# Message passes of a graph network: a subtraction split over two engines, gathers spaced by arithmetic, one root for two norms

## The reference, cut to what matters

```
for l in range(3):
    m = concat([x[dst], x[src], edge_features])
    m = relu(layernorm(m @ msg_w1[l] + msg_b1[l]))
    m = relu(layernorm(m @ msg_w2[l] + msg_b2[l]))
    agg = segment_sum(m, dst)
    x = x + relu(layernorm(concat([x, agg]) @ upd_w[l] + upd_b[l]))
```

## Time and profile before

| | |
|---|---|
| Device time, median of 3 runs | 12204.72 us (12200.19 to 12210.75) |
| Span of the profiled execution | 10931.0 us |
| Busy: TensorE, VectorE, ScalarE, GpSimd | 68%, 58%, 57%, 68% of the span |
| The three message passes, from the span's start | about 3215 to 4375, 4735 to 5830, 6200 to 7275 us |

### The profile page before, as it was taken

One profiled execution on the slowest core, in us unless ns is written; L12 is line 12 of the kernel. 1 busy time (PEld: TensorE's weight loads), 2 busy tenths in 40 slices (PEclk: granted clock), 3 DMA queues, 4 the chain that ended last, 5 costly groups with the idle time before them and its releaser, 6 DMA issues. The chain is left out here.

```text
span 10931.0 us, 359225 instructions
## 1 busy us (share of the span) xinstructions
PE 7478.6 (68%) x118837; PEld 6235.2 (57%) x118838; DVE 6352.6 (58%) x16271; ACT 6235.4 (57%) x16925; POOL 7430.6 (68%) x9327
## 2 busy tenths in 40 slices
PE   6666666555687777777777877767777756445666
PEld 5444444344576666766666766656666643443465
DVE  7444444455438888357774477763488887116543
ACT  2555555555449999368884488862499966003200
POOL 2777777777558887468885588860288854773576
PEclk8555555555699999899998999989999989668877
DMA  6222222189996666675555855559966649887998
GB/s 239 69 65 70 69 66 69 60 291 320 270 330 204 202 203 182 251 248 170 170 168 176 306 170 170 170 86 373 345 201 201 201 146 394 259 259 271 358 331 251
DMA packets 1258845, 2290.57 MB, mean 210 GB/s; under 512 B 293739, under 2 KB 691324, under 8 KB 1231742
## 3 DMA queue, kind: packets, MB, share of 16 engines
q1 hardware_dynamic: 913886, 1129.25, 32.5%
q0 software_dynamic: 232416, 575.55, 17.9%
q10 hardware_dynamic: 112320, 582.80, 13.1%
HBM read 1381.15 MB, written 905.59 MB: 209 GB/s over the span
## 5 line engine op out<-in xcount | busy, mean ns | idle before, releaser
L639 POOL DMA_INDIRECT by_src<-sort_rec,slots x1560 | 1540.9, 988 | 651.2 <-issue 650.9
L1312 POOL DMA_INDIRECT NEAR<-spread_f,gather_ids_l x1368 | 1322.5, 967 | 336.9 <-issue 252.8
L1387 ACT ACTIVATE z_l<-z_l,stat_l 128x64 f32<-128x64 f32 x5472 | 1438.0, 336 | 0.0
L773 PE MATMUL bank<-hots_t 104*128 104x512 bf16 (+3 forms) x1568 | 612.6, 466 | 722.0 <-ACT junk L598 721.7
L1475 PE MATMUL bank<-m_l,NEAR 128*128 128x64 bf16 x5472 | 559.0, 193 | 517.7 <-issue 391.4
L1475 PEld LDWEIGHTS bank<-m_l,NEAR 128*128 128x128 bf16 x5472 | 492.8, 97 | 561.8 <-issue 552.5
L1321 POOL TENSOR_TENSOR rest_l<-m_l 128x512 f32<-128x512 f32 x684 | 716.0, 1047 | 140.5 <-DVE m_l L1375 130.7
L1487 PE MATMUL bank<-wm_diag,zr_t_l 128*128 128x128 f32 x5472 | 807.3, 291 | 0.0
L773 PEld LDWEIGHTS bank<-hots_t 104*128 104x128 bf16 x1568 | 217.3, 139 | 1021.0 <-ACT junk L598 833.8
L1487 PEld LDWEIGHTS bank<-wm_diag,zr_t_l 128*128 128x128 f32 x5472 | 674.9, 194 | 156.8 <-issue 156.8
L1301 POOL TENSOR_TENSOR piece_l<-rest_l 128x512 bf16<-128x512 f32 x684 | 710.9, 1039 | 59.9 <-POOL rest_l L1321 12.2
(11 more groups left out here) (379 smaller groups left out, 25591.5 us busy)
## 6 DMA issues: line engine op xcount, KB each, us to landing
spread_f<-unit_rows_a ACTq DMA_DIRECT2D x342, 512.0 KB, 5.8
hot_t_l<-dst_hots_t SPq DMA_DIRECT2D x456, 256.0 KB
NEAR<-dst_hots SPq DMA_DIRECT2D x456, 256.0 KB, 3.2
unit_hot_a<-src_hots_t SPq DMA_DIRECT2D x342, 256.0 KB, 4.1
spread<-sum_unit_rows ACTq DMA_DIRECT2D x114, 768.0 KB
spread<-last_unit_rows ACTq DMA_DIRECT2D x114, 768.0 KB
dst_hots<-NEAR SPq DMA_DIRECT2D x228, 256.0 KB, 2.5
dst_hots_t<-hot_t_l SPq DMA_DIRECT2D x228, 256.0 KB, 2.1
```

Of the source, the lines that this page charges most:

```text
L639: pool.indirect_dma_start(out=by_src, out_offset=bass.IndirectOffsetOnAxis(ap=slots[h][:, j:j + 1], axis=0), in_=rec[h][:, j, :], in_offse ...
L773: pe.matmul(to, lhsT=cols[:, t * P:width], rhs=cols[:, 0:width], start=True, stop=False, skip_group_check=True)
L1312: pool.indirect_dma_start(out=far_in[h % WA][:, g * GT:(g + 1) * GT, :].rearrange("p j f -> p (j f)"), out_offset=None, in_=spread_f, in_o ...
L1387: last = act.activation(z[h % WA][:, t, :], z[h % WA][:, t, :], ACT.Relu, scale=stat[h % WA][:, 2, t:t + 1])
```

## The change

In `mpnn_pass` alone:

- `piece2` is split by columns: VectorE does the first 256 (4 tiles), between the second norm's sum and the keys, GpSimd the other 256. TensorE waits for both.
- GpSimd's order becomes gather, half of `piece2`, ids, gather, `rest`.
- The sums of both norms go to one array `sizes`; one root and one reciprocal a tick serve the first norm of lag 4 and the second norm of lag 8. VectorE's reciprocal at the head of the tick goes. The array's second column is set to 1.0 ahead of the pass.

```diff
 GpSimd
+                        if p := part(0):
+                            h, st, n, nth = p
+                            if h % WA == 0:
+                                pool.wait_ge(s["ids"], 2 * nth - (h < WA))
+                            at_least(pool, s["z"], n - WA)
+                            pool.sem_inc(turn, 1)
+                            gather(h, 0)
                         if p := part(9):
                             h, st, n, nth = p
                             pool.wait_ge(s["rest"], n)
                             at_least(pool, s["acc_ps"], n - 2)
-                            pool.tensor_tensor(piece2[h % 2][:], rest[h % 2][:], top(rest[h % 2]),
+                            pool.tensor_tensor(piece2[h % 2][:, LOW:, :], rest[h % 2][:, LOW:, :], top(rest[h % 2])[:, LOW:, :],
                                                ALU.subtract).then_inc(s["piece2"], 1)
                         if p := part(0):
                             h, st, n, nth = p
-                            if h % WA == 0:
-                                pool.wait_ge(s["ids"], 2 * nth - (h < WA))
-                            at_least(pool, s["z"], n - WA)
                             if h % WA == WA - 1 and not (isinstance(st, int) and st + 1 >= steps):
                                 take_ids(1 - h // WA, st + 1)
                             pool.sem_inc(turn, 1)
-                            for g in range(2):
-                                pool.indirect_dma_start(
...
+                            gather(h, 1)
 VectorE
+                    for k in range(WA):
+                        dve.memset(sizes[k][:, 0, 1, :], 1.0).then_inc(s["sized"], 1)
+                    dve.wait_ge(s["sized"], WA)
...
-                        if p := part(5):
-                            h, st, n, nth = p
-                            dve.wait_ge(s["root1"], n)
-                            dve.reciprocal(stat[h % WA][:, 2, :], stat[h % WA][:, 1, :]).then_inc(s["rec1"], 1)
...
                         if p := part(8):
                             h, st, n, nth = p
                             dve.wait_ge(s["square2"], n)
-                            dve.tensor_reduce(stat[h % WA][:, 3, :], vv[:], AX, ALU.add).then_inc(s["sum2"], 1)
+                            dve.tensor_reduce(sizes[h % WA][:, 0, 1, :], vv[:], AX, ALU.add).then_inc(s["sum2"], 1)
+                        if p := part(9):
+                            h, st, n, nth = p
+                            dve.wait_ge(s["rest"], n)
+                            at_least(dve, s["acc_ps"], n - 2)
+                            dve.tensor_tensor(piece2[h % 2][:, 0:LOW, :], rest[h % 2][:, 0:LOW, :], top(rest[h % 2])[:, 0:LOW, :],
+                                              ALU.subtract).then_inc(s["piece2_v"], 1)
...
+                        if p := norms(part):
+                            h, k, n = p
+                            dve.wait_ge(s["root"], k)
+                            dve.reciprocal(sizes[h % WA][:, 2, :, :], sizes[h % WA][:, 1, :, :]).then_inc(s["rec"], 1)
 ScalarE
-                        if p := part(8):
-                            h, st, n, nth = p
-                            act.wait_ge(s["sum2"], n)
-                            act.activation(stat[h % WA][:, 4, :], stat[h % WA][:, 3, :], ACT.Sqrt, bias=eps[:],
-                                           scale=1.0 / D).then_inc(s["root2"], 1)
-                        if p := part(4):
-                            h, st, n, nth = p
-                            act.wait_ge(s["sum1"], n)
-                            act.activation(stat[h % WA][:, 1, :], stat[h % WA][:, 0, :], ACT.Sqrt, bias=eps[:],
-                                           scale=1.0 / D).then_inc(s["root1"], 1)
+                        if p := norms(part):
+                            h, k, n = p
+                            act.wait_ge(s["sized"], WA)
+                            act.wait_ge(s["sum1"], min(k, steps) if isinstance(k, int) else k)
+                            at_least(act, s["sum2"], n)
+                            act.activation(sizes[h % WA][:, 1, :, :], sizes[h % WA][:, 0, :, :], ACT.Sqrt, bias=eps[:],
+                                           scale=1.0 / D).then_inc(s["root"], 1)
 TensorE
                             pe.wait_ge(s["piece2"], n)
+                            pe.wait_ge(s["piece2_v"], n)
```

More of the change, by code:

```diff
@@ L1238, in mpnn_pass @@
             piece2 = lb("piece2", [P, 2 * GT, D], BF16, 2)
-            stat = lb("stat", [P, 6, 2 * GT], F32, WA)
+            sizes = lb("sizes", [P, 3, 2, 2 * GT], F32, WA)
+            LOW = GT
             s = {n: sem(f"{n}_l{l}") for n in (
-                "key", "hot", "turned", "hot_t", "near", "z", "square1", "sum1", "root1", "rec1", "relu", "relu_turned",
-                "relu_t", "v_ps", "square2", "sum2", "root2", "rec2", "message", "rest", "piece2", "acc_ps", "acc_first",
-                "acc_added", "ids")}
+                "key", "hot", "turned", "hot_t", "near", "z", "square1", "sum1", "relu", "relu_turned", "relu_t", "v_ps",
+                "square2", "sum2", "root", "rec", "message", "rest", "piece2", "piece2_v", "acc_ps", "acc_first", "acc_added",
+                "ids", "sized")}
             rec_in = [sem(f"rec_in{h}_l{l}") for h in range(WB8)]
@@ L1259, in top, with norms @@
                 return x_[:].bitcast(BF16)[:, :, 1:2 * D:2]
+            def norms(part):
+                if p := part(4):
+                    return p[0], p[2], p[2] - WA
+                if p := part(8):
+                    return p[0], p[2] + WA, p[2]
             with nc.Block() as block:
@@ L1294, in take_ids, with gather @@
                         pool.tensor_copy(gather_ids[k][:], run_ids[:, bass.ds(2 * first_step, 2 * WA)]).then_inc(s["ids"], 1)
-                    def tick(part):
-                        if p := part(9):
-                            h, st, n, nth = p
-                            pool.wait_ge(s["rest"], n)
-                            at_least(pool, s["acc_ps"], n - 2)
-                            pool.tensor_tensor(piece2[h % 2][:], rest[h % 2][:], top(rest[h % 2]),
-                                               ALU.subtract).then_inc(s["piece2"], 1)
+                    def gather(h, g):
+                        pool.indirect_dma_start(
+                            out=far_in[h % WA][:, g * GT:(g + 1) * GT, :].rearrange("p j f -> p (j f)"),
+                            out_offset=None, in_=spread_f, in_offset=bass.IndirectOffsetOnAxis(
+                                ap=gather_ids[h // WA][:, 2 * (h % WA) + g:2 * (h % WA) + g + 1], axis=0),
+                        ).then_inc(far_ready[h % WA], 16)
+                    def tick(part):
                         if p := part(0):
@@ L1307, in tick @@
                             at_least(pool, s["z"], n - WA)
+                            pool.sem_inc(turn, 1)
+                            gather(h, 0)
+                        if p := part(9):
+                            h, st, n, nth = p
+                            pool.wait_ge(s["rest"], n)
+                            at_least(pool, s["acc_ps"], n - 2)
+                            pool.tensor_tensor(piece2[h % 2][:, LOW:, :], rest[h % 2][:, LOW:, :], top(rest[h % 2])[:, LOW:, :],
+                                               ALU.subtract).then_inc(s["piece2"], 1)
+                        if p := part(0):
+                            h, st, n, nth = p
                             if h % WA == WA - 1 and not (isinstance(st, int) and st + 1 >= steps):
@@ L1347, in tick @@
                             dve.wait_ge(s["square1"], n)
-                            dve.tensor_reduce(stat[h % WA][:, 0, :], zz[:], AX, ALU.add).then_inc(s["sum1"], 1)
+                            dve.tensor_reduce(sizes[h % WA][:, 0, 0, :], zz[:], AX, ALU.add).then_inc(s["sum1"], 1)
                         if p := part(8):
@@ L1387, in scaled_relu @@
                             last = act.activation(z[h % WA][:, t, :], z[h % WA][:, t, :], ACT.Relu,
[L1388 removed]
+                                                  scale=sizes[h % WA][:, 2, 0, t:t + 1])
                         return last
```

12 lines of the change are left out of this document (5 added, 7 removed).

## The result

The changed kernel takes 12341.1 us (median of 4 runs, 12299.2 to 12386.8), the kernel before 12207.7 in the same comparison (12200.2 to 12227.1): ratio 1.0106, interval 1.0071 to 1.0141, so 1.1% slower. The forecast was 12230; its rival "GpSimd always comes first" said 12335, the upper end of the range.

The account below looks back on a forecast made before the run. The first pass was taken as bound by a one-step ring (4.97 us), later passes by GpSimd (4.55). Span 10931.0 + 105 - 82 + 2 = 10956, plus 1273.7, gave 12230 us; range 12125 to 12335.

Parts of the forecast that it names:

- GpSimd always comes first: Later passes: if VectorE is over 0.07 later, GpSimd leads every step; step 4.68, cost 23 us, total 12335; chance 0.20.
- 105 - 82 + 2: Span sum in us: first pass costs 105, later passes gain 82, memsets ahead of the passes cost 2.
- What bounds the kernel: Message pass: a one-step ring of 4.97 us bounds the first pass, GpSimd's own 4.55 the later ones.
- the ring over keys and one-hots: First pass: square, sum, keys, one-hots, TensorE's transposes and products, back to the next square: 4.97 us a step.
- Costs of the parts: GpSimd's half 0.63 us, VectorE's 0.42, gap after arithmetic 0.15; the joint root worth nothing.
- The rival without holding: Halves don't hold each other: first pass 5.31 a step, later 4.20, with 0.07 4.27; total 12119 us; chance 0.12.
- The hold: Overlapping halves: the second comer is held; VectorE's ends 0.28 after GpSimd's, or GpSimd's takes 0.91.
- First pass, +105 said: First pass: held VectorE half lengthens the ring from 4.97 to 5.43 us, costing 0.46 x 228 = 105 us.
- Later passes, -82 said: Later passes: engines take turns coming first, step 4.45 instead of 4.63, gaining 0.18 x 456 = 82 us.
- Case A: Later passes: GpSimd's half first, VectorE's held to 0.91; VectorE's next half ready at 4.54, GpSimd's at 4.61.
- B: Later passes: VectorE's half comes first by 0.07 and holds GpSimd's to 0.91; the step after is Case A again.
- The 1273.7 us held over the span: Difference between the 12204.7 median and the profiled span, kept constant and added to the forecast span of 10956.

Follow-up runs that it names:

- the operand in PSUM: Changed kernel, but VectorE's half takes its second input from a zero-filled PSUM bank instead of SBUF; ratio 0.9969 to the kernel before.
- with one semaphore: Changed kernel, but both halves count up one semaphore and TensorE waits once; ratio 1.0074 to the kernel before.
- the clock back: Changed kernel with 16 useless matmuls per first-pass step ahead of TensorE's wait for the one-hots; ratio 1.0107 to the kernel before.
- The order alone: Kernel before with the whole subtraction on GpSimd moved between the two gathers, nothing given to VectorE, two roots; ratio 1.0062 to the kernel before.
- the split alone: Kernel before with the subtraction split, GpSimd's half right behind `rest`, VectorE's half behind the second sum, two roots; ratio 0.9980 to the kernel before.
- the keys first: Kernel before with keys and one-hots ahead of the second norm's sum on VectorE in the first pass; ratio 1.0018 to the kernel before.

## Why the prediction was wrong

In the experiments the change adds 152 us (133 in the first comparison), where the sum had 105 - 82 + 2 = 25. The steps, one by one:

- **What bounds the kernel: right.** ScalarE was not the bound of the first pass (one root fewer changed nothing: 1131.5 against 1132.2), the ring over keys and one-hots was. GpSimd was the bound of the later ones: its freed gap alone gives 37 a pass.
- **Costs of the parts: right.** GpSimd's half 0.62 (0.63 said), VectorE's 0.41 (0.42), the gap after arithmetic 0.16 (0.15), the joint root nothing. The rival without holding was sized right too: it said 5.31 and 4.20, and with the operand in PSUM, where nothing is held, 5.30 and 4.21 were measured.
- **The hold: right, in both directions.** VectorE's half ends 0.29 after GpSimd's (0.28 said). GpSimd's, when it is the one held, ends 0.88 after VectorE's start (5206.45 to 5207.33 with one semaphore; 0.91 said). The operand in PSUM ends the hold. First pass, ring 5.43 said, median step 5.49.
- **First pass, +105 said, +145 measured: a term was missing.** The clock. It was read as 1.00 in the earlier trace rows and taken as given. With steps half a microsecond longer, TensorE is 748 instead of 775 of 1000 us busy and is granted 0.93; the tail of long steps costs 29 us (1277.6 - 1248.6). The rest, 11 us, is 0.05 a step: with the clock back the mean step is 5.50, so 0.51 over the 4.99 of the kernel before, where 0.46 was forecast; no run takes this apart. The order alone fell to 0.93 as well, and the split alone to 0.95.
- **Later passes, -82 said, +8 measured: the step that failed.** Case A has "TensorE starts at 0.96": VectorE's half ends at 0.91, and 0.05 was left for TensorE to restart. The earlier trace rows show 0.07 there (5308.15 + 1.04 to 5309.26), with one semaphore for the whole subtraction; the change gives TensorE two waits, and with VectorE last it starts 0.227 after it: at 1.14. Then the square comes at 3.48, and VectorE's next half is ready at 4.72, not 4.54. GpSimd's is there at 4.61, so it comes first again, and its ring of 4.61 is the step: median 4.65, and 4.68 said for this rival. With one semaphore the gap is 0.071, the turns come back, and the mean step is 4.45, as the forecast had it. GpSimd is not first always, though: in 30 of the 228 steps of the second pass VectorE is, in the main in one of every eight. Shorter steps around these (down to 4.36) bring the mean to 4.62, which is why the two passes lose 8 us and not the rival's 23.
- **The weights.** The forecast said itself that B rests on a lead of 0.07 and named the two new waits as what could use it up, yet gave that rival 0.20. That its 12335 lies near the measured 12341 is in part luck: it had +105 and +23, where the experiments have +145 and +8. A lead smaller than any cost that the change itself adds to that path decides nothing, and this cost was to be bounded from both sides as a term of its own, which it was not.
- **The 1273.7 us held over the span.** They are not time outside the span: the changed kernel's profiled run of 12299.2 us is 1.7 longer than its span. They are the distance between the two kinds of times. Most of that distance lies ahead of the first pass, whose first square comes at 4081.7 in the changed kernel's first profile and at 3237.0 in the profile before. The sum was not hurt much by it, since the change costs nearly the same in both.

The change costs time, then, because in the first pass it puts 0.34 of work and 0.12 of holding on a ring that had no slack, and in the later passes it moves GpSimd's subtraction to where the two halves meet. The part that gains, half of the subtraction away from the engine that is the bound, gains where it is put behind `rest` and left out of the first pass.

What stays open: why two waits cost 0.16 more than one when the later event is the second wait's. The runs show the gap with either, not what TensorE does in it. The last 11 us of the first pass stay open too.

## What to carry to other kernels

Where a step repeats, work out not only how long an operation is held but who is first next time; if that hangs on less than a tenth of a microsecond, bound each wait that the change adds before giving the case a weight. An operation moved between engines must be placed by what the other engine reads at that moment: the same half subtraction gained 64 us a pass behind `rest` and, with two waits, nothing behind a gather, where it met VectorE's half. Ask per stage who gains: here the split pays in two passes of three, and the version that leaves the first alone takes 1.1% off.

## What the runs showed of the hardware

- **Two waits ahead of a matmul.** In the later passes TensorE's first load comes 0.227 after VectorE's end, in the median, where that is the second of two semaphores. It comes 0.07 after it where there is one, and 0.07 to 0.12 after GpSimd's end where GpSimd, the first of the two, is last.
- **A gather is held too.** An indirect gather that starts while VectorE makes the one-hots (two inputs from SBUF, 0.69 long) takes 1.47 in the median and not 0.95, ending 0.84 after them (195 of them in the first pass with the keys first). One-hots that start inside a running gather keep their 0.69. The Trainium skill ("SBUF — State Buffer", "Who interferes with whom") infers, for the descriptors of DMAs that GpSimd issues, that a `tensor_tensor` does not stall them. These indirect gathers, which also read their row numbers from SBUF, are held by one all the same, and the measurement decides; what in the gather is held is not shown.
- **A held operation ends a fixed time after its holder.** Of 32 columns it ended 0.06 after it, of 256 0.29, and this was 0.28 to 0.29 whether VectorE's half started 0.2 or 0.6 before GpSimd's end. In the last 0.1 of the holder it is not held: in this step of the split alone VectorE starts 0.09 before GpSimd's end and takes 0.41.

```profile
5201.15 0.61 POOL L1302 TENSOR_TENSOR piece_l<-rest_l 128x256 bf16<-128x256 f32 x1
```

```profile
5201.67 0.41 DVE L1358 TENSOR_TENSOR piece_l<-rest_l 128x256 bf16<-128x256 f32 x1
```

- **A longer wait in a step came with a lower clock.** With TensorE waiting 0.5 us longer in each step, its granted clock was 0.93 in the mean of the pass instead of 1.00. In one of the long steps it was 0.51 while the eight loads of the second product took 1.78 instead of 0.97. Work of no use ahead of the wait brought back 1.00 and 29 us.
